# q and k as 64 real rows per channel, four channels side by side on TensorE, and an inverse on four row groups

## The reference

```
x = x + L0(_gn(x))        # depthwise 3x3 with weights from an attention over 4 kernels, then 1x1 (32 -> 32)
x = x + L1(_gn(x))
# L1:
hidden = einsum('oc,bchw->bohw', w_hidden, x)          # 32 -> 192 channels
hidden = depthwise_3x3(hidden, w_dw)
q, k, v = split(hidden, 3)                             # 64 channels each
q_fft, k_fft = rfft2(to_patch(q)), rfft2(to_patch(k))  # patches of 8 x 8
out = irfft2(q_fft * k_fft)
out = layer norm of out over the 64 channels, times norm_w plus norm_b
L1 = einsum('oc,bchw->bohw', w_out, v * out)           # 64 -> 32
```

## Time and profile before

| | |
|---|---|
| median of 3 runs | 2588.41 us (2576.62 to 2591.29) |
| profiled execution | 2588.67 us, its span 2586.9 us |
| busy | PE 2465.4, PEld 1644.8, DVE 1638.6, ACT 1432.4, POOL 476.5 us |
| granted TensorE clock, mean of the span | 0.972 |
| chain that ended last | PE 76% of the span |

### The profile page before, as it was taken

How to read it: one execution, slowest core, us unless ns; L and a number is a source line. 1 busy time by engine, 2 the same in 40 slices (tenths; PEclk the granted TensorE clock), 3 DMA queues, 4 the chain that set the end, 5 groups by cost and what they waited for, 6 DMA issues and landing times.

```text
span 2586.9 us, 90657 instructions
## 1 busy us (share of the span) xinstructions
PE 2465.4 (95%) x40199; PEld 1644.8 (64%) x40199; DVE 1638.6 (63%) x4058; ACT 1432.4 (55%) x2381; POOL 476.5 (18%) x324
## 2 busy tenths in 40 slices
PE   6888988969999999999999999999999999999998
PEld 3333333357777777777777777777777777777775
DVE  3566766536666666666666666666666666666665
ACT  3455656555555555555555555555555555555552
POOL 1000000002222222222222222222222222222222
PEclk9888889879999999999999999999999999999999
DMA  7588898762222222222222222222222222233222
GB/s 139 147 210 214 219 237 215 195 155 69 68 69 69 69 69 68 69 69 69 69 68 69 69 69 69 68 69 69 69 69 68 69 69 68 71 74 74 72 52 50
DMA packets 60345, 248.30 MB, mean 96 GB/s; under 512 B 12393, under 2 KB 12658, under 8 KB 53714
## 3 DMA queue, kind: packets, MB, share of 16 engines
q1 hardware_dynamic: 59954, 242.50, 38.5%
HBM read 140.74 MB, written 101.72 MB: 94 GB/s over the span
## 4 chain that ended last, share of the span: by engine, by line
PE 76%; issue 1%; ACT 1%; DVE 0%; SPq 0%; DMA 0%; ACTq 0%
PE bank L575 21%; PE bank L652 18%; PE bank L668 10%; PE bank L558 9%; PE bank L635 8%; PE bank L588 6%; PE bank L597 4%; ACT arena L821 1%; SPq L318 0%; DMA xn_d<-arena 0%; DVE arena L1110 0%; DVE arena L961 0%; ACT arena L866 0%; DVE arena L1198 0%; DVE arena L1135 0%
## 5 line engine op out<-in xcount | busy, mean ns | idle before, releaser
L441 POOL TENSOR_TENSOR arena<-arena 128x8 f32<-128x8 f32 x256 | 452.2, 1766 | 1585.1 <-DVE arena L1116 1580.1
L575 PE MATMUL bank<-arena 128*64 128x512 f16 x4608 | 689.3, 393 | 0.0
L812 ACT ACTIVATE arena<-bank 100x512 f32<-100x512 f32 x1024 | 604.2, 628 | 95.8 <-PE bank L558 74.4
L1198 DVE TENSOR_TENSOR arena<-bank,arena 128x512 f32<-128x512 f32 x512 | 352.8, 691 | 432.3 <-PE bank L652 352.4
L652 PE MATMUL bank<-arena 100*64 100x128 f32 x8192 | 511.6, 274 | 13.7 <-issue 7.0
L652 PEld LDWEIGHTS bank<-arena 100*64 100x64 f32 x8192 | 455.9, 136 | 52.6 <-issue 45.6
L558 PEld LDWEIGHTS bank<-arena 128*36 128x36 f16 (+1 forms) x8192 | 327.8, 104 | 228.0 <-ACT arena L812 12.7
L512 PE MATMUL bank<-arena 32*32 32x508 f32 (+1 forms) x9216 | 391.7, 665 | 52.6 <-issue 37.7
L558 PE MATMUL bank<-arena 128*36 128x128 f16 (+1 forms) x8192 | 388.9, 220 | 11.0 <-DVE arena L1100 4.2
L858 ACT ACTIVATE arena<-bank 128x512 f32<-128x512 f32 x256 | 149.3, 598 | 343.8 <-PE bank L635 261.7
L821 ACT ACTIVATE arena<-bank,arena 128x256 f32<-128x256 f32 x512 | 261.0, 560 | 128.5 <-PE bank L588 127.9
(11 more groups left out here) (112 smaller groups left out, 1624.1 us busy)
## 6 DMA issues: line engine op xcount, KB each, us to landing
arena<-xn_d SPq DMA_DIRECT2D x128, 536.2 KB, 8.2
xn_d<-arena SPq DMA_DIRECT2D x130, 260.0 KB, 4.5
x_d<-arena SPq DMA_DIRECT2D x64, 512.0 KB, 8.3
arena<-x_d SPq DMA_DIRECT2D x128, 256.0 KB, 4.9
out<-arena SPq DMA_DIRECT2D x128, 256.0 KB, 5.4
arena<-x_in SPq DMA_DIRECT2D x32, 544.0 KB, 10.1
arena<-x_in SPq DMA_DIRECT2D x32, 528.0 KB, 10.0
arena<-spectra_in SPq DMA_DIRECT2D x1, 1152.0 KB
```

Of the source, the lines that this page charges most:

```text
L441: pool.tensor_tensor(tiny["rstd"][:, slot], tiny["var_eps"][:, slot], powers, ALU.pow).then_inc(s_root, 1)
L575: mm = pe.matmul(v_banks[chunk % 3][64 * s:64 * s + 64, :], v_w[:, 64 * tap:64 * tap + 64], at(xs[half], row * WP + 32 * k + dx, [32 * WP, ...
L812: act.activation(h_rows[0:WIN, :, first:first + 4], banks[g % ring][0:WIN, :].rearrange("p (i c) -> p c i", i=4), ACT.Copy).then_inc(s_h_r ...
L1198: dve.tensor_tensor(parts(prod[m % 3][:, 512 * second:512 * second + 512]), parts(k_banks[n % 3]), q_sb[m % 2][:, 256 * second:256 * secon ...
```

## The change

Of the 64 frequencies of a real 8 x 8 patch, 30 pairs are mirror images and 4 are their own mirror. q and k are each held as 64 real numbers: 32 rows (the cosine parts of the 30 pairs and two of the self-mirrored) and 32 more (the sine parts of the pairs and the other two). Both halves of a channel are put on the same 32 partitions, one behind the other in the columns, and four channels lie side by side on the 128 partitions. `G_k` shrinks from 128 to 64 columns per channel, `spectra` from 3072 to 1024 columns, and 16 matmuls build the tables in place of 24.

- q: 16 matmuls of 32 columns per octet in place of 8 of 64; k: 16 of 32 columns in place of 16 of 64. Four of them stand on the four column quarters.
- The product has four parts (each half of k times each half of q); DVE still makes 16 of 128 x 512 per unit, but begins after a whole octet of k.
- The inverse contracts 32 rows per channel four times (`both`): 32 matmuls of 32 rows, 64 columns, 256 moving columns per pair of octets, in place of 16 of 64 rows. Four row groups and two column halves, each row group with a PSUM bank of its own; ACT takes it out in four copies of 256 columns.
- The banks are dealt anew: one bank for q (two before), two for k, four for the inverse. `inverse(e)` waits until all copies of `inverse(e - 1)` are made (`y_ready`), and `inverse(2)` and `inverse(3)` stand one behind the other at the unit's end.
- The tail's last gate on DVE moves behind the first two products, its residual behind the fourth, its copy-out on ACT behind the first copy of q, its projection on TensorE one octet on.

```diff
-TABLES = {"tables": (("identity", 128), ("inverse", 128), ("w_out", 64)),
+TABLES = {"tables": (("identity", 128), ("inverse", 256), ("w_out", 64)),
...
-            for y in range(8):
-                for x in range(8):
-                    a = 2 * np.pi * ((u * y + v * x) % 8) / 8
-                    spectra[3 * dy + dx, :, :, y + dy, x + dx] = [np.cos(a), np.sin(a), np.cos(a) + np.sin(a)]
...
+    u, v = np.divmod(np.arange(64), 8)
+    mirror = 8 * (-u % 8) + -v % 8
+    real = np.flatnonzero(mirror == np.arange(64))
+    pairs = np.flatnonzero(mirror > np.arange(64))
+    freq = np.concatenate([pairs, real[:2], pairs, real[2:]])
+    sine = (np.arange(64) >= 32) & (np.arange(64) < 32 + len(pairs))
+    angle = 2 * np.pi * ((u[freq][:, None] * u + v[freq][:, None] * v) % 8) / 8
+    wave = np.where(sine[:, None], np.sin(angle), np.cos(angle)).reshape(64, 8, 8)
...
+    inverse = np.concatenate([np.where(paired, 2, 1) * cosines[:32], np.where(paired, 2 * sines[:32], 0), np.where(paired, 2 * sines[:32], 0),
+                              np.where(paired, -2, 1) * cosines[32:]], axis=1) / 64
+    out["inverse"] = np.tile(inverse, (4, 1)).astype(np.float32)
...
-        v_banks = [banks[3], banks[5], banks[7]]
-        k_banks = [banks[2], banks[3], banks[4]]
-        i_banks = [banks[5], banks[7]]
+        ring_banks = [banks[1], banks[3], banks[7]]
+        v_banks = [banks[2], banks[5], banks[0]]
+        q_bank = banks[0]
+        k_banks = [banks[1], banks[2]]
+        i_banks = [banks[3], banks[5], banks[7], banks[4]]
...
-        spectra, row_mask = x2[2][:, 0:3072], x2[2][:, 3072:3584]
+        spectra, row_mask = x2[2][:, 0:1024], x2[2][:, 1024:1536]
...
-        prod = [take(1024) for _ in range(3)]
+        prod = take(4 * 1024)
...
-                for m in range(24 * step // 18, 24 * (step + 1) // 18):
-                    if m % 16 == 0:
-                        pe.wait_ge(s_taps, m // 16 + 1)
+                for m in range(16 * step // 18, 16 * (step + 1) // 18):
+                    if m % 8 == 0:
+                        pe.wait_ge(s_taps, m // 8 + 1)
                     if m > 3:
                         pe.wait_ge(s_g_ready, m - 3)
-                    pe.matmul(banks[m % 4], spectra[0:96, 128 * m:128 * m + 128], taps[m // 16][0:96, :],
+                    pe.matmul(banks[m % 4], spectra[0:96, 128 * (m % 8):128 * (m % 8) + 128], taps[m // 8][0:96, :],
                               start=True, stop=True).then_inc(s_g_mm, 1)
...
-                if g < 2 and positive(8 * u):
-                    pe.wait_ge(s_q_copied, 8 * u)
-                if ring == 4 and g == 1:
+                if g in (1, 2) and positive(16 * u):
+                    pe.wait_ge(s_y_ready, 16 * u - (3, 1)[g - 1])
...
-                    pe.wait_ge(s_prod_ready, 16 * u + 14)
-                if chunk in (1, 2):
-                    pe.wait_ge(s_y_ready, 8 * (u + 1) - 2 + chunk)
+                    pe.wait_ge(s_prod_ready, 16 * (u + 1))
+                if chunk == 1:
+                    pe.wait_ge(s_y_ready, 16 * (u + 1) - 2)
+                if chunk == 2:
+                    pe.wait_ge(s_q_copied, 8 * (u + 1))
...
-                    if positive(8 * u + m - 1):
-                        pe.wait_ge(s_q_copied, 8 * u + m - 1)
-                    for pair in range(4):
-                        for par in range(2):
-                            ch = 8 * m + 2 * pair + par
-                            mm = pe.matmul(banks[m % 2][64 * par:64 * par + 64, 128 * pair:128 * pair + 128],
-                                           G_q[0:WIN, 64 * ch:64 * ch + 64], hwin[0:WIN, 128 * ch:128 * ch + 128], start=True, stop=True)
+                    if positive(8 * u + m):
+                        pe.wait_ge(s_q_copied, 8 * u + m)
+                    for quad in range(2):
+                        for part in range(2):
+                            for c in range(4):
+                                ch, first = 8 * m + 4 * quad + c, 256 * quad + 128 * part
+                                mm = pe.matmul(q_bank[32 * c:32 * c + 32, first:first + 128],
+                                               G_q[0:WIN, 64 * ch + 32 * part:64 * ch + 32 * part + 32],
+                                               hwin[0:WIN, 128 * ch:128 * ch + 128], start=True, stop=True)
                     mm.then_inc(s_q_mm, 1)
-                def k_quad(n, octet=None):
-                    if positive(16 * u + n - 2):
-                        pe.wait_ge(s_prod_ready, 16 * u + n - 2)
-                    if n == 1 and tail is not None:
+                def k_octet(m):
+                    if positive(16 * u + 2 * m - 2):
+                        pe.wait_ge(s_prod_ready, 16 * u + 2 * m - 2)
+                    if m == 1 and tail is not None:
                         pe.wait_ge(s_gated, 8 * u - 1)
-                    if n == 2 and tail is not None:
-                        pe.wait_ge(s_t_copied, 8 * u)
-                    for pair in range(2):
+                    for quad in range(2):
                         for part in range(2):
-                            if octet is not None and pair == 1 and part == 1:
-                                inverse_inputs(octet)
-                            for par in range(2):
-                                ch = 4 * n + 2 * pair + par
-                                mm = pe.matmul(k_banks[n % 3][64 * par:64 * par + 64, 256 * part + 128 * pair:256 * part + 128 * pair + 128],
-                                               G_k[0:WIN, 128 * ch + 64 * part:128 * ch + 64 * part + 64],
+                            for c in range(4):
+                                ch, first = 8 * m + 4 * quad + c, 256 * quad + 128 * part
+                                mm = pe.matmul(k_banks[m % 2][32 * c:32 * c + 32, first:first + 128],
+                                               G_k[0:WIN, 64 * ch + 32 * part:64 * ch + 32 * part + 32],
                                                hwin[0:WIN, 128 * (64 + ch):128 * (64 + ch) + 128], start=True, stop=True)
                     mm.then_inc(s_k_mm, 1)
 
-                def inverse_inputs(m):
-                    pe.wait_ge(s_prod_ready, 16 * u + 2 * m + 2)
-                    if positive(8 * u + m - 1):
-                        pe.wait_ge(s_y_ready, 8 * u + m - 1)
-                    if m == 1 and tail is not None:
+                def inverse(e):
+                    pe.wait_ge(s_prod_ready, 16 * u + 4 * e + 4)
+                    if positive(16 * u + 4 * e):
+                        pe.wait_ge(s_y_ready, 16 * u + 4 * e)
+                    if e == 0 and tail is not None:
                         pe.wait_ge(s_gated, 8 * u)
-
-                def inverse_octet(m):
-                    for part in range(2):
-                        for par in range(2):
+                        pe.wait_ge(s_t_copied, 8 * u)
+                    for both in range(4):
+                        for c in range(4):
                             for lam in range(2):
-                                mm = pe.matmul(i_banks[par][64 * lam:64 * lam + 64, 256 * (m % 2):256 * (m % 2) + 256],
-                                               small["inverse"][64 * par:64 * par + 64, 64 * part:64 * part + 64],
-                                               at(prod[m % 3][64 * par:64 * par + 64, :], 256 * part + 64 * lam, [512, 2], [128, 2], [1, 64]),
-                                               start=part == 0, stop=part == 1)
+                                mm = pe.matmul(i_banks[c][64 * lam:64 * lam + 64, 256 * (e % 2):256 * (e % 2) + 256],
+                                               small["inverse"][32 * c:32 * c + 32, 64 * both:64 * both + 64],
+                                               at(prod[32 * c:32 * c + 32, :], 2048 * (e % 2) + 128 * both + 64 * lam, [512, 4], [1, 64]),
+                                               start=both == 0, stop=both == 3)
                     mm.then_inc(s_inverse_mm, 1)
 
                 pe.wait_ge(s_h_ready, 32 * (u + 1))
...
+                    k_octet(m)
                     if m < 7:
                         q_octet(m + 1)
-                    if m in (2, 4, 6):
-                        k_quad(2 * m, m - 1)
-                        inverse_octet(m - 2)
-                        inverse_octet(m - 1)
-                    else:
-                        k_quad(2 * m)
-                    k_quad(2 * m + 1)
-                    if m == 0 and tail is not None:
+                    if m == 1 and tail is not None:
                         project(tail, 3)
-                pe.wait_ge(s_prod_ready, 16 * u + 14)
-                pe.wait_ge(s_y_ready, 8 * u + 6)
-                inverse_octet(6)
-                pe.wait_ge(s_prod_ready, 16 * u + 16)
-                inverse_octet(7)
+                    if m in (2, 4):
+                        inverse(m // 2 - 1)
+                inverse(2)
+                inverse(3)
                 v_chunk(u, half, 0, 0, 0, None)
...
```

(41 more changed lines are left out.)

51 lines of the change are left out of this document (24 added, 27 removed).

## The result

The change makes the kernel slower: 2663.81 us, median of 4 runs (2654.66 to 2669.22), against 2584.86 us for the kernel before in 4 runs (2576.62 to 2591.29), a ratio of 1.0304 [1.0258, 1.0349]. Forecast were 2445 us and a range of 2425 to 2560. The profiled execution took 2667.07 us, its span 2665.3, with a mean granted clock of 0.940 (0.972 before).

The account below looks back on a forecast made before the run. TensorE was taken to bound the kernel, its spectral part being 29.2 us per unit. Terms summed to -4.25 us per unit, 136 us over 32 units, 144 with the opening: 2588.67 to 2445 us, range 2425 to 2560.

Parts of the forecast that it names:

- Covered: Work taken as hidden behind TensorE, at no cost: DVE's products, ACT's longer copies (+1.1 us per unit) and SP's loads.
- k and q: Octet matmuls of 32 columns run four abreast, 0.89 us per octet: k saves 6.9 us per unit, q costs 0.15.
- Inverse: Inverse blocks: 64 records in place of 32, eight abreast, as many sets of 219 ns; +0.1 us per block, +0.4 per unit.
- The wait in front of the last inverse: TensorE waits before `inverse(3)` for ACT's four copies of 128 x 256: 1.5 us per unit, bounds 1.3 and 2.3.
- Changes of shape: Around the tail's projection the tile shape now changes before and after: 0.15 us an edge, +0.3 us per unit.
- One bank for q: The next q octet waits for ACT's copy of the last, partly covered by k: +0.3 us per unit, bounds 0 and 0.9.
- The opening: Table building before the convolution: eight fp32 matmuls fewer and less to load, 8 us saved, bounds 4 and 11.
- the likeliest case: Whole kernel: small squares overlap and the summed terms hold, 2445 us, bounds 2425 to 2490; chance 0.66.
- Rival 1: The clock falls in the new wait before the last inverse: 2460 to 2605 us, most likely about 2500; chance 0.16.
- Rival 2: Small squares in octets and inverse run at the convolution's 34 ns per record, not 27: 2583 us, no change; chance 0.09.
- Rival 3: The inverse's eight squares load or run four at a time, 3.5 us per block: 2669 us, slower; chance 0.06.
- Rival 4: Matmuls of 32 columns in q and k still pass two by two, 1.75 us per octet: 2886 us; chance 0.03.

## Why the prediction was wrong

**The step that failed** is a sentence under *Covered*, priced at nothing: "The loads of SP begin at the same place." They do. What changed is what happens beneath them. Under that burst TensorE has to be fed with instructions, and the change halves the time in which it eats a packet, from 7.0 to 3.5 us. It cost 158.4 us of issue idle, and the clock behind it: a mean of 0.96 from 600 to 2600 us, with only 1.00 and 0.50 granted, means 8% of 2000 us at half speed, which loses some 75 us, an estimate (80, less the part in which TensorE stood still anyway). Together some 235 of the 250 us between the change (2663.8) and the same change with its transfers spread (2413.4). No rival named it. The hints were in what I had read: 1.61 us of `<-issue` amid dense work in stage 2, which I used for its clock alone, without asking what it was (it ends 1.4 us behind the landing of a packet of instructions, at 1452.6 us, under a burst); and the queue of instructions, in the page from the start.

**The rest of the sum held.** It is read from the change with spread transfers, since nothing else of TensorE's was altered there. Its timeline:

```profile
1013.71 1.08 PE L683 MATMUL bank<-arena 100*32 100x128 f32 x32
1014.61 1.06 PE L669 MATMUL bank<-arena 100*32 100x128 f32 x32
...
1016.38 1.08 PE L669 MATMUL bank<-arena 100*32 100x128 f32 x32
1017.40 1.08 PE L630 MATMUL bank<-arena 128*64 128x512 f32 x4
1018.41 1.08 PE L683 MATMUL bank<-arena 100*32 100x128 f32 x32
...
1020.29 2.00 PE L698 MATMUL bank<-arena 32*64 32x256 f32 x64
1022.22 1.08 PE L683 MATMUL bank<-arena 100*32 100x128 f32 x32
...
1033.06 2.00 PE L698 MATMUL bank<-arena 32*64 32x256 f32 x64
1036.52 2.21 PE L698 MATMUL bank<-arena 32*64 32x256 f32 x64 [1.47 <-ACT arena L888]
1038.66 2.25 PE L608 MATMUL bank<-arena 128*64 128x512 f16 x18
```

- *k and q*: 0.87 to 0.90 us per 32 records; 0.89 forecast.
- *Inverse*: 1022.22 - 1020.29 = 1.93 us per block; 1.91 before, and 0.1 more forecast. Eight squares do run abreast: 64 records in 1.93 us, 30 ns each. The Trainium skill's rule for weight loads (TensorE: Matmul & The Clock Gate, section LDWEIGHTS) would have had 53 ns per load, 3.4 us per block; the measurement decides against its use one load at a time for these squares of different rows. For q and k, whose loads have 32 columns, the same rule gives 27 ns, which is the pace measured; whether loads or matmuls set the pace there is not shown.
- *The spectral part*: 1038.66 - 1013.71 = 24.95 us; 25.0 forecast.
- *The wait in front of the last inverse*: 1.47 us; 1.5 forecast. ACT's copy of 128 x 256 took 390 ns, 365 estimated, and four of them in the changed kernel 1.21 us, 1.16 estimated.
- *Changes of shape*: the q group ahead of the projection takes 1017.40 - 1016.38 = 1.02 us, the projection 1018.41 - 1017.40 = 1.01, each 0.15 us above its pace; +0.3 us, as forecast.
- *One bank for q*: no wait of q for ACT's copy of it stands among PE's waits; the 0.3 us per unit were not there.
- *The opening*: 10.2 us earlier; 8 forecast. PE timeline of the kernel after, to be held against 51.63 in the earlier trace rows, and the load of the tables against 1152 KB in the earlier trace rows:

```profile
41.42 5.50 PE L519 MATMUL bank<-arena 32*32 32x512 f32 x160 [0.69 <-ACT arena L771]
...
arena<-spectra_in SPq DMA_DIRECT2D x1, 384.0 KB
```

- *The whole*: spread against spread, the change is worth 2571.66 - 2413.35 = 158 us; 144 forecast. Between their two traces (154 us), 139 lie in stage 2, where 136 were forecast, and 15 ahead of it (it begins at 513.8 and at 499.0 us). The forecast's sum held but for one thing that it left out, which was larger than all of it.
- *The bounds*: the errors listed for the likeliest case add up to 88 us upwards, so to 2533; the 2490 comes out only if they are added as squares (44 us), which the prediction doesn't say, and the lower bound of the wait (1.3 us) is missing from them.

**The rivals.** *Rival 1* named the clock, which did fall, but not for its reason: with the 1.5 us wait in every unit and no stalls it stays at 1.00. Where the prediction was unsure between 1.16 us of idle with a fall and 1.61 us without one, these waits of 1.47 us behind dense work side with the latter; the length of the pause alone does not decide it. *Rival 2*, 34 ns per record, is refuted by 27 ns. *Rival 3* had 2669 us, and the result is 2664; that is chance, since its mechanism (3.5 us per inverse block) is refuted by 1.93. *Rival 4* is refuted by the octets. A number that agrees is no evidence without its place in the trace.

**Open.** The bytes in flight and the appetite for instructions make the stall together; that is shown from both sides. The packet that ends the stall above is itself as quick as others (1.4 us, where the median of 381 is 1.1), so it waits before it starts to move; whether TensorE asks late or the DMA engines answer late, no view shows. Of the last 15 of the 250 us, 5 lie ahead of stage 2, which begins at 504.1 us in the change and at 499.0 with the spread; the others have no place. That the stall is what lowers the clock rests on the two going and coming together in all runs.

## What to carry to other kernels

Cutting matmuls into smaller tiles cost nothing on the array here and doubled the instructions per microsecond: count them (here from 27 to 14 ns each), find the largest burst of transfers that they run under, and look in the DMA part of the page at the queue of instructions. Idle time `<-issue` in the middle of a group, between matmuls that have no wait, was missing instructions here, and each restart came 1.2 to 1.7 us behind the landing of a packet; spread the transfers in small pieces over the unit before giving up a denser stream. And when a wait is moved away, ask first who else would have been late at that place: here a wait for ACT of 1.47 us became one for DVE of the same length.

## What the runs showed of the hardware that I had not expected

- TensorE's instructions come in packets of 16 KB, 256 instructions, through a DMA queue of their own, and a burst of 2.1 MB on another queue, at 0.94 and 0.74 of the DMA engines' time, holds TensorE up for as much as 6 us at an appetite of 14 ns per instruction. At 27 ns per instruction, the same burst costs 7.6 us in 1700, against 135.2.
- It is the bunching: with 77 GB/s in small pieces the stall is 4.2 us, with 68 GB/s in bursts 135.2.
- After a stall of 5.35 us the clock came back to 2.4 GHz within about 6 us of dense work: the groups at 1150.52 and 1152.23 pass at half speed, the block at 1153.85 at full.
